# Block 0's one-hots on VectorE: one tensor_scalar per chunk in place of one tensor_tensor per half look-up

## The reference

```python
e = stack([tbl_f[ids[:, f]] for f in range(26)], axis=1)         # 2048 x 26 x 128
combined = concatenate([dense[:, None, :], e], axis=1)           # 2048 x 27 x 128
inter = einsum('bfd,bgd->bfg', combined, combined)[:, iu0, iu1]  # 351 pairs, each once
z = concatenate([dense, inter, dense], axis=1)                   # 2048 x 607
h = maximum(z @ W_top1 + b_top1, 0)                              # 512
h = maximum(h @ W_top2 + b_top2, 0)                              # 256
y = h @ W_top3                                                   # 2048 x 1
```

## Time and profile before

| | |
|---|---|
| median of 3 runs | 379.87 us (377.62 to 384.15) |
| span of the profiled execution | 496.1 us (its own device time is not given) |
| mean granted TensorE clock | 0.904 |
| TensorE matmul busy | 376.0 us |
| VectorE busy | 244.4 us |
| ScalarE busy | 195.0 us |
| GpSimd busy | 254.8 us |

### The profile page before, as it was taken

One profiled execution on the slowest core, in us unless ns is written; L12 is line 12 of the kernel. 1 busy time (PEld: TensorE's weight loads), 2 busy tenths in 40 slices (PEclk: granted clock), 3 DMA queues, 4 the chain that ended last, 5 costly groups with the idle time before them and its releaser, 6 DMA issues.

```text
span 496.1 us, 8109 instructions
## 1 busy us (share of the span) xinstructions
PE 376.0 (76%) x3360; PEld 301.4 (61%) x3360; DVE 244.4 (49%) x174; ACT 195.0 (39%) x261; POOL 254.8 (51%) x266
## 2 busy tenths in 40 slices
PE   1951777858586665978798796969788696879997
PEld 1630656647474554767586666867676455666787
DVE  4740789674919370765725750956566101112133
ACT  3810986414242521525252532434354334344400
POOL 6774540655737363646666554747466564730000
PEclk9985799989989796989998898989899898789899
DMA  8841763259915153456714533536232621123330
GB/s 210 218 134 41 218 187 85 70 156 275 227 29 161 45 155 103 109 150 153 183 46 128 160 87 104 143 93 193 74 89 63 168 73 27 49 63 100 69 71 5
DMA packets 38479, 58.44 MB, mean 118 GB/s; under 512 B 21665, under 2 KB 22561, under 8 KB 38444
## 3 DMA queue, kind: packets, MB, share of 16 engines
q1 hardware_dynamic: 29304, 40.74, 30.3%
q0 software_dynamic: 8192, 16.79, 13.5%
q10 hardware_dynamic: 948, 0.41, 0.4%
HBM read 47.68 MB, written 10.23 MB: 117 GB/s over the span
## 4 chain that ended last, share of the span: by engine, by line
PE 58%; issue 16%; DVE 11%; another core or an unknown queue 8%; SPq 3%; DMA 2%; ACT 2%; DVEq 0%; ACTq 0%
PE look_bank L727 25%; PE short_bank L821 15%; DVE one_hot L1031 8%; PE out_bank L757 6%; PE out_bank L771 4%; PE short_bank L806 4%; PE out_bank L766 3%; SPq L632 2%; DVE all_combined L1044 1%; DVE low_table L1019 1%; DMA spread_ids<-in_ids_by_feature 1%; PE out_bank L783 1%; SPq L621 1%; DMA last_scratch<-all_dots 1%
## 5 line engine op out<-in xcount | busy, mean ns | idle before, releaser
L682 POOL DMA_INDIRECT rows<-in_tbl,all_ids x256 | 253.9, 992 | 191.9 <-PE short_bank L821 81.9
L1031 DVE TENSOR_TENSOR one_hot<-spread_ids,row_bank 128x2048 fp32r<-128x2048 int32 (+3 forms) x80 | 170.7, 2175 | 27.1 <-PE look_bank L727 10.7
L727 PE MATMUL look_bank<-one_hot,high_table 125*128 125x512 f32 x328 | 140.8, 429 | 20.0 <-issue 16.1
L727 PE MATMUL look_bank<-one_hot,low_table 125*128 125x512 f32 x328 | 132.4, 404 | 0.6 <-issue 0.6
L821 PE MATMUL short_bank<-all_combined 128*59 128x54 f32 x2048 | 88.1, 247 | 53.2 <-issue 51.5
L821 PEld LDWEIGHTS short_bank<-all_combined 128*59 128x59 f32 x2048 | 79.7, 162 | 66.7 <-issue 66.5
L1044 DVE COPY all_combined<-short_bank 128x512 f32<-128x512 f32 x32 | 21.8, 691 | 156.2 <-PE short_bank L806 122.3
L727 PEld LDWEIGHTS look_bank<-one_hot,high_table 125*128 125x128 f32 x328 | 64.5, 197 | 40.5 <-issue 23.6
L727 PEld LDWEIGHTS look_bank<-one_hot,low_table 125*128 125x128 f32 x328 | 64.6, 197 | 16.9 <-issue 4.1
L925 ACT COPY all_dots<-short_bank 128x432 f32<-128x432 f32 x64 | 33.1, 518 | 97.1 <-remote 53.7
L878 ACT COPY looked_up<-look_bank 128x512 f32<-128x512 f32 x40 | 23.4, 586 | 120.8 <-remote 45.3
(11 more groups left out here) (42 smaller groups left out, 183.5 us busy)
## 6 DMA issues: line engine op xcount, KB each, us to landing
whole_table<-in_tbl SPq DMA_DIRECT2D x26, 448.0 KB
spread_ids<-in_ids_by_feature SPq DMA_DIRECT2D x40, 256.0 KB
block_scratch<-all_dots SPq DMA_DIRECT2D x24, 208.0 KB
rows<-in_tbl,all_ids POOLq DMA_INDIRECT x256
block_scratch<-all_dots SPq DMA_DIRECT2D x24, 104.0 KB
pairs<-block_scratch SPq DMA_DIRECT2D x72, 29.2 KB
whole_table<-in_tbl SPq DMA_DIRECT2D x26, 52.0 KB
whole_table<-in_tbl SPq DMA_DIRECT2D x2, 560.0 KB
```

Source lines behind the costliest of these rows:

```text
L682: nc.gpsimd.indirect_dma_start(rows[:, t % ROW_TILES, slot, :], None, tables[SLOT_FEATURES[slot]][:, :], bass.IndirectOffsetOnAxis(ap=all_ ...
L727: last = nc.tensor.matmul(look_bank[s % LOOK_BANKS][:], table_parts[part][TABLE_PLACE[s]][0:ROWS_K, c, :], one_hot[0:ROWS_K, (chunks_befor ...
L1031: last = nc.vector.tensor_tensor(one_hot[:, place:place + n, :], spread_ids[:, s % ID_PLACES:s % ID_PLACES + 1, :].to_broadcast([P, n, COLS]),
```

## The change

In block 0 (`s < FIRST_LOOK[1]`, the first ten looks) VectorE makes a half chunk by chunk: a tensor_scalar compares the 512 ids in SBUF with one number per partition, the chunk's column of `chunk_row` in SBUF, and writes one 128x512 place. Later blocks, ScalarE's halves, the semaphores and all orders stay as they are.

```diff
-                for c, n, place in runs_of(s, h):
+                if s < FIRST_LOOK[1]:
+
+                    for c in halves(s)[h]:
+                        last = nc.vector.tensor_scalar(
+                            one_hot[:, (chunks_before(s) + c) % HOT_PLACES, :], spread_ids[:, s % ID_PLACES, :],
+                            chunk_row[CHUNKS[s]][:, c:c + 1], None, ALU.is_equal)
+                for c, n, place in runs_of(s, h) if s >= FIRST_LOOK[1] else []:
                     last = nc.vector.tensor_tensor(
                         one_hot[:, place:place + n, :], spread_ids[:, s % ID_PLACES:s % ID_PLACES + 1, :].to_broadcast([P, n, COLS]),
                         bank_row(CHUNKS[s])[:, c:c + n].unsqueeze(2).to_broadcast([P, n, COLS]), ALU.is_equal)
```

## The result

The changed kernel takes 388.21 us (median of 4 runs, 384.74 to 388.36) against 380.76 us of the kernel before: 1.0194 times as long (95% interval 1.0131 to 1.0257), 7.4 us slower. The forecast, 380.4 us, lies outside that interval; the measured time is inside the range of 375.5 to 390, and near the 386 us of the first rival.

What follows compares the result with a forecast made beforehand. ScalarE was taken to bound the opening looks, TensorE the rest. VectorE's 3.4 us of added work, mostly absorbed by its waits, was put between −1 and +1 us; +0.5 us on 379.87 gave 380.4 us, range 375.5 to 390.

Steps and rivals of the forecast that it cites:

- the first rival: Block 0: gathers wait for the new instructions, lengthening GpSimd's stream; 10 us of hold-up gives 386, 20 gives 396; chance 0.19.
- What bounds the kernel: ScalarE bounds the opening looks, VectorE following; afterwards TensorE bounds, GpSimd's gathers close behind, starting 1.25 us apart.
- The prediction's slack sum: GpSimd's gather stream: 335.5 us, plus 7 us waiting and 2.1 us to land, 344.6, against last transposes at 348.2.
- about 4 us: Hold-up of GpSimd's gathers from which their stream was to decide the kernel's time.
- The cost of the new instruction: Block 0's 58 tensor_scalars on VectorE: 0.69 us each, 0.61 us in a row, together 3.4 us more work.
- Where it goes on VectorE and ScalarE: Block 0's looks: VectorE mostly waits for ScalarE's high part, so added or saved work nets −1 to +1 us; +0.5 taken.
- gathers held up: Block 0: new SBUF-to-SBUF instructions hold GpSimd's gathers; 10 us, up to 35 us more stream; chance 0.19, 0.08 beyond +2%.
- the forecast's own mechanism: Nothing changes because the new form is no faster in block 0; 379 to 381.5 us, chance 0.60.
- the Trainium skill's rule: Two-port tensor_scalar holds the port pair GpSimd needs to write DMA descriptors; two-input instructions hold only GpSimd's reads; 6 to 24 us.
- The prediction's own sign of being wrong: Gathers in block 0 run to 1.2 us and more, and GpSimd no longer waits for tile 1's products.
- VectorE held up by the gathers: New instructions wait for what a gather holds; at 0.8 us each 389.5, at 1.25 us over 400; chance 0.09.
- VectorE was the bound: TensorE's 3.7 and 1.8 us waits are real VectorE time; cheap instructions return up to 5.5 us: 374.5; chance 0.12.

Runs made afterwards that it cites:

- the unstretched kernel: The kernel before, no edit, profiled once more for an execution that is not stretched: span 378.7 us, 381.12 us timed.
- the run with a wait between: Against the changed kernel, VectorE waits on a semaphore for each tensor_scalar of a half to end before starting the next: 382.30 us, 1.0053 to the kernel before.
- where the stream has room: Kernel before and changed kernel, each with one gather in four left out from tile 2 on (56 of 256): 373.70 us and 375.19 us.

## Why the prediction was right or wrong

**What bounds the kernel: wrong, and this is the step that failed.** "After that TensorE bounds, with GpSimd's gathers close behind" was read from a stretched execution, in which GpSimd waited 81.9 us for pair products. Unstretched it waits 1.0 us for them, and the gathers bound the kernel from 3 us on. The prediction's slack sum had the right form, and its terms were taken from the stretched execution. The stretch of the gathers, 12.2 us there, is 21.9 in the unstretched kernel (an explanation that was not tested: gathers and subtractions meet more often when GpSimd never rests). The 7 us of waiting for tile 0's products are 1.0, which leaned the other way and makes up for 6 of these 9.7 us; the 3.7 us that are left are the whole slack of the sum. The 31.7 us from the last transposes to the end are 31.2 (347.50 to 378.7). Measured: 3.1 us to the first gather, 256 x 0.944 us, 21.9 us of stretch and 78.4 us of idleness between gathers give 345.1 us for the end of the last gather, and its four transposes start 2.4 us later, without slack. The "about 4 us" were none. Two readings of the stretched trace lean the same way: the 51.5 us of the earlier trace rows are less than half of the 116 us that they are said to hold most of, and the earlier trace rows puts VectorE's 1.70 us before 61.54 us down to "issue", not to ScalarE.

**The cost of the new instruction: mis-sized.** 0.61 us in a row was taken, 0.40 measured; 3.4 us more VectorE work was forecast, and VectorE's busy time fell by 8.3 us (243.6 to 235.3). The row of the same width was a two-input instruction, and not the nearest in kind. The estimate of 0.42 us for a single pass, worked out from the Trainium skill ("VectorE: DVE Perf Modes", section "The perf-mode tier table"), was nearer to the 0.48 us measured than the 0.69 us taken.

**Where it goes on VectorE and ScalarE: right that it gives nothing.** Of the 8.3 us, 6.3 appear as longer waits for ScalarE's high parts (11.0 us in total before, 17.3 with the change), and the time does not fall.

**The rival "gathers held up": right in kind.** Its two shapes were one wait for the rest of an instruction per gather (10 us) and a gather that never gets in (up to 35 us). The first is the usual one (11 gathers get in with the row still going on), and the second happened to one gather in a row of nine. 15.1 − 3.9 = 11.2 us of extra hold on the first 32 gathers stand beside its 10 us, and 388.2 beside its 386. That the numbers are so near is in part luck: it took 3.6 us off for slack that was not there, while in fact 4.6 us were given back after the opening. The measured time lies in the stated range because the range was made wide enough for this rival, not because the forecast's own mechanism held. The rival was given 0.19. The argument against it, that the pattern "needs two SBUF inputs", was refuted by the changed kernel's own trace; the two forms with ids from SBUF and rows from SBUF hold, the form with rows from PSUM does not. The two long gathers that the prediction counts as agreeing with the Trainium skill's rule lay under subtractions with two SBUF inputs, and said nothing of a tensor_scalar; its estimates for this rival, 6 and 24 us, enclose the 11.2. The prediction's own sign of being wrong came true: gathers in block 0 run to 1.2 us and more, and GpSimd waits for no products.

**The rival "VectorE held up by the gathers": not seen in the changed kernel.** The 58 instructions have a mean of 482 ns with a gather beside each, and only one lasts 0.64 us. That the mechanism exists shows where gaps let gathers in first (the run with a wait between).

**The rival "VectorE was the bound": not seen**; the first pair products came 3.5 us later, not sooner. They are late (63.1 to 65.1 us) in all kernels in which tile 0's gathers are held, and on time (60.0 to 61.1 us) in all others. What links the two was read from the trace, not tested alone. The last turn of tile 0 starts at 33.40 us, after TensorE has waited 2.39 us for a landing, only 0.6 us later than before (32.77 us). But TensorE's granted clock is then 0.50 from 34.1 to 36.4 us (1.2 GHz; its matmuls last 0.63 us instead of 0.39), and again from 57.0 to 60.0 us, behind a wait of 2.05 us for ScalarE; in the kernel before it is 1.00 (2.4 GHz) in both stretches. Behind the stream all this costs little: 1.5 us, with intervals that overlap, where the stream has room.

## What to carry to other kernels

Before costing an edit, ask of each engine's stream whether it ever rests, in an execution that lasts about as long as the timed ones; a profile 116 us over the median hid that GpSimd never did. Where GpSimd issues gathers without rest, what VectorE does beside them is judged by what it holds and not only by its length: here one SBUF input and one in PSUM held no gather, while two SBUF inputs or a tensor_scalar within SBUF did. Keep the small operand in PSUM where the form allows it; cut a long two-input instruction in two; leave a gap between tensor_scalars that follow each other.

## What the hardware showed that was not expected

- A gather (0.94 us) that starts under a tensor_tensor with two SBUF inputs waits for its end and then takes some 0.82 us more; behind a tensor_scalar within SBUF it takes only 0.12 us more. What part of a gather waits in either case is not shown. Moving the 8 or 10 columns of row numbers from PSUM to SBUF for 14 halves cost 15 us of 380.
- Nine tensor_scalars that followed each other at once held one gather for 4.66 us, though most gathers got in earlier (1.28 us for one wholly inside a row of eight); with a semaphore wait between them gathers of 0.94 to 0.98 us pass.
- The 128x512 tensor_scalar (int32 in, fp32r out, one fp32 number per partition) took 0.48 us, the tensor_tensor of the same size, rows in PSUM, 0.69 us; in a row they come every 0.40 and 0.60 us.
